# A fused attention and gated feed-forward kernel: the fillings between attention steps dealt anew, and three element-wise jobs moved from VectorE to GpSimd

## What is computed

```
paths  = sigmoid(x @ Wp + bp)                      # 8 heads x 5 values
agree  = pq * pk + (1 - pq) * (1 - pk)
sim    = cumprod(agree, -1).sum(-1) / 5, causal    # 1024 x 1024 per head
x1     = layernorm(x + softmax(sim) @ (x @ Wv) @ Wo)
h      = silu(x1 @ wg.T) * (x1 @ wu.T)             # hidden width 768
out    = layernorm(x1 + h @ wd.T)
```

## Time and profile before

| what | us |
|---|---|
| median of three runs | 982.97 |
| lowest and highest | 975.43, 983.63 |
| the profiled execution's own time | 978.61 |
| its span, first to last instruction | 976.9 |

### The profile page before, as it was taken

The page is one execution under the profiler, slowest core; times in us unless marked ns, Lnnn a source line. Parts: engine busy times, 40 slices in busy tenths (PEclk is TensorE's granted clock), DMA queues, the critical chain, the costliest instruction groups (busy, mean ns, idle before and its releaser), DMA issues.

```text
span 976.9 us, 13193 instructions
## 1 busy us (share of the span) xinstructions
PE 793.5 (81%) x4866; PEld 379.8 (39%) x4866; DVE 737.0 (75%) x1164; ACT 459.7 (47%) x721; POOL 327.3 (34%) x265
## 2 busy tenths in 40 slices
PE   5377798898879889789888889778988888789764
PEld 3133244342533435243443426334443434243332
DVE  2848878779678787797687796797787887788643
ACT  2235554646356454545445463554546463545221
POOL 0010262245324262152512462152622444253412
PEclk9578999999999999999999999999999999999877
DMA  6831443121421424104431415204411224100000
GB/s 206 216 78 52 87 87 108 44 66 44 108 87 44 108 62 108 68 12 97 87 108 44 87 43 121 68 29 108 88 65 44 49 61 108 44 1 22 1 22 23
DMA packets 44338, 70.94 MB, mean 73 GB/s; under 512 B 3568, under 2 KB 21232, under 8 KB 44272
## 3 DMA queue, kind: packets, MB, share of 16 engines
q1 hardware_dynamic: 44272, 70.07, 27.3%
HBM read 53.28 MB, written 16.78 MB: 72 GB/s over the span
## 4 chain that ended last, share of the span: by engine, by line
PE 46%; DVE 21%; issue 11%; ACT 10%; POOL 9%; DMA 2%; SPq 0%; DVEq 0%; ACTq 0%; POOLq 0%
PE misc L808 9%; PE ctx_ps L755 8%; ACT probs L422 7%; PE slot L735 7%; PE misc L711 6%; PE misc L798 6%; PE misc L775 5%; POOL probs L365 5%; DVE acc L508 4%; DVE work L586 4%; POOL work L374 3%; DVE x L569 2%; DVE acc L511 2%; DVE bn L558 2%; PE misc L720 2%
## 5 line engine op out<-in xcount | busy, mean ns | idle before, releaser
L422 ACT ACTIVATE probs<-slot 128x1024 f32<-128x1024 f32 (+3 forms) x384 | 290.3, 809 | 339.9 <-PE slot L735 262.2
L511 DVE TENSOR_TENSOR acc<-acc,probs 128x2048 f32<-128x2048 f32 (+3 forms) x128 | 221.4, 1730 | 5.3 <-POOL probs L365 4.8
L374 POOL TENSOR_TENSOR work<-work 128x512 f16<-128x512 f32 x96 | 145.3, 1514 | 208.8 <-ACT work L440 208.5
L365 POOL TENSOR_SCALAR_AFFINE_SELECT probs<-probs 128x512 f32<-128x512 f32 x128 | 132.5, 1037 | 244.2 <-ACT probs L422 244.2
L735 PE MATMUL slot<-query_stack,key_stack 128*128 128x512 f16 (+3 forms) x768 | 164.4, 337 | 24.9 <-DMA query_stack<-phi_dram 15.2
L755 PE MATMUL ctx_ps<-probs,vz_sb 128*32 128x512 f32 (+3 forms) x1536 | 175.4, 531 | 2.6 <-POOL probs L365 2.6
L798 PE MATMUL misc<-x1T_hi,w_parts 128*128 128x512 f16 x384 | 148.6, 387 | 21.5 <-DVE work L586 15.8
L798 PE MATMUL misc<-x1T_lo,w_parts 128*128 128x512 f16 x384 | 147.5, 384 | 0.0
L735 PEld LDWEIGHTS slot<-query_stack,key_stack 128*128 128x128 f16 x768 | 57.6, 99 | 207.1 <-issue 150.0
L808 PE MATMUL misc<-w_parts,work 128*128 128x256 bf16 x768 | 98.6, 290 | 22.4 <-POOL work L374 22.2
L370 POOL TENSOR_TENSOR rstd<-var_eps,neg_half 128x4 f32<-128x4 f32 x32 | 51.1, 1597 | 182.7 <-DVE var_eps L563 159.2
(11 more groups left out here) (54 smaller groups left out, 636.6 us busy)
## 6 DMA issues: line engine op xcount, KB each, us to landing
key_stack<-phi_dram SPq DMA_DIRECT2D x64, 256.0 KB, 5.8
query_stack<-phi_dram SPq DMA_DIRECT2D x64, 256.0 KB, 6.7
xT_sb<-in_xT_dram SPq DMA_DIRECT2D x8, 1024.0 KB, 5.0
x_sb<-in_x_dram SPq DMA_DIRECT2D x8, 1024.0 KB, 5.6
out_dram<-x SPq DMA_DIRECT2D x16, 512.0 KB, 2.9
phi_dram<-phi_hi SPq DMA_DIRECT2D x16, 256.0 KB, 2.1
phi_dram<-phi_lo SPq DMA_DIRECT2D x16, 256.0 KB, 2.4
work<-in_wgT_dram SPq DMA_DIRECT2D x1, 768.0 KB, 8.2
```

What stands on the lines that cost most here:

```text
L365: pool.affine_select(out=tile, in_=tile, compare_op=ALU.is_ge, fill=0.0, base=0, pattern=[[0, 4], [1, P]], channel_multiplier=-1).then_inc ...
L374: pool.tensor_tensor(hid_lo[:, n % M1, :], hid[:, n % HSLOTS, :], hid_hi[:, n % M1, :], ALU.subtract).then_inc(hid_lo_ready, 1)
L422: act.activation(probs[:, s % P_SLOTS, 2 * p:2 * p + 2, off:CH], slot[p][:, :, off:CH], ACT.Exp).then_inc(slot_drained[p], 1)
L511: dve.tensor_tensor(acc[:, :, off:CH], acc[:, :, off:CH], own, ALU.add).then_inc(summed, 1)
```

## The change

The table `BETWEEN` is rewritten, and `bias`, `features` and `apply` move from VectorE's program to GpSimd's, in the same form of instruction. Since `features` now shares no engine with what follows `turn_f`, it gains a wait, for the transposes of the sample before. The gate pairs stood in steps 7 to 10, 12, 13 and 17 to 22; they now stand in 0 to 2, 12 to 15, 17, 18 and 21 to 23.

```diff
-        0: [("stack", 0, 1)] + down(-1, 0, 0),
-        1: down(-1, 0, 1) + norm(1, -1, 0),
-        2: vz(1, 0, 1, 2) + [("apply", 1, -1, 0), ("store", -1, 0)],
-        3: project(-1, 1) + norm(0, -1, 1),
-        4: vz(1, 3, 4, 5) + [("load_x", 0), ("apply", 0, -1, 1), ("bias", 1, 0), ("squash", 1, 0)],
-        5: vz(1, 6, 7) + [("features", 1, 0)],
-        6: turn_x1(-1, 1) + [("load_xT", 2), ("bias", 1, 1), ("squash", 1, 1)]
-            + turn_f(1, 0, 0) + turn_f(1, 1, 0) + [("features", 1, 1)],
-        7: gate_pair(-1, 6),
-        8: gate_pair(-1, 7) + halves(-1, 6) + turn_f(1, 0, 1) + [("phi_store", 1, 0)],
-        9: gate_pair(-1, 8) + halves(-1, 7) + turn_f(1, 1, 1) + [("phi_store", 1, 1)],
-        10: gate_pair(-1, 9) + halves(-1, 8),
-        11: project(0, 0) + halves(-1, 9) + norm(0, 0, 0),
-        12: gate_pair(-1, 10) + [("apply", 0, 0, 0)],
-        13: gate_pair(-1, 11) + halves(-1, 10),
-        14: turn_x1(0, 0) + halves(-1, 11),
-        15: down(-1, 1, 0),
-        16: [("stack", 1, 0)] + down(-1, 1, 1) + norm(1, -1, 1),
-        17: gate_pair(0, 0) + [("apply", 1, -1, 1), ("store", -1, 1)],
-        18: gate_pair(0, 1) + halves(0, 0),
-        19: gate_pair(0, 2) + halves(0, 1),
-        20: gate_pair(0, 3) + halves(0, 2),
-        21: gate_pair(0, 4) + halves(0, 3),
-        22: gate_pair(0, 5) + halves(0, 4),
-        23: halves(0, 5),
+        0: [("stack", 0, 1)] + gate_pair(-1, 3) + halves(-1, 2),
+        1: gate_pair(-1, 4) + halves(-1, 3),
+        2: gate_pair(-1, 5) + halves(-1, 4),
+        3: vz(1, 0, 1) + halves(-1, 5),
+        4: project(-1, 1) + norm(0, -1, 1),
+        5: down(-1, 0, 0) + [("apply", 0, -1, 1)],
+        6: down(-1, 0, 1) + norm(1, -1, 0),
+        7: vz(1, 2, 3) + [("load_x", 0), ("bias", 1, 0), ("squash", 1, 0), ("apply", 1, -1, 0), ("store", -1, 0)],
+        8: turn_x1(-1, 1) + vz(1, 4) + [("features", 1, 0)],
+        9: vz(1, 5, 6),
+        10: vz(1, 7) + turn_f(1, 0, 0) + turn_f(1, 1, 0)
+            + [("load_xT", 2), ("bias", 1, 1), ("squash", 1, 1), ("features", 1, 1)],
+        11: project(0, 0) + norm(0, 0, 0),
+        12: gate_pair(-1, 6) + [("apply", 0, 0, 0)],
+        13: gate_pair(-1, 7) + halves(-1, 6),
+        14: gate_pair(-1, 8) + halves(-1, 7),
+        15: gate_pair(-1, 9) + halves(-1, 8),
+        16: turn_f(1, 0, 1) + turn_f(1, 1, 1) + halves(-1, 9) + [("phi_store", 1, 0), ("phi_store", 1, 1)],
+        17: [("stack", 1, 0)] + gate_pair(-1, 10),
+        18: gate_pair(-1, 11) + halves(-1, 10),
+        19: turn_x1(0, 0) + halves(-1, 11) + down(-1, 1, 0),
+        20: down(-1, 1, 1),
+        21: gate_pair(0, 0) + norm(1, -1, 1),
+        22: gate_pair(0, 1) + halves(0, 0) + [("apply", 1, -1, 1), ("store", -1, 1)],
+        23: gate_pair(0, 2) + halves(0, 1),
...
+            def features(b, h):
+                rows = slice(HT * H * h, HT * H * (h + 1))
+                pool.wait_ge(u_ready, 2 * b + h + 1)
+                if b == 0:
+                    pool.wait_ge(consts_ready, 3)
+                else:
+
+                    for g in range(NG):
+                        k, n = MISC["turn_f", b - 1, g, h]
+                        pool.wait_ge(misc_filled[k], n + 1)
+                for m in range(DEPTH):
+                    w = 2 ** m
+                    if m >= 1:
+                        pool.wait_ge(feat_ready, DEPTH * (2 * b + h) + m)
+                    pool.tensor_tensor(feat[:, rows, w:2 * w], feat[:, rows, 0:w],
+                                      u_sb[:, rows, m:m + 1].to_broadcast([P, HT * H, w]),
+                                      ALU.mult).then_inc(feat_ready, 1)
+
+            def apply(ln, b, c):
+                pool.wait_ge(rstd_ready, NORM[ln, b, c] + 1)
+                for t in range(TC):
+                    row = x1[:, TC * c + t, :]
+                    pool.tensor_scalar(row, row, mv[:, t, 0:1], rstd[:, t:t + 1],
+                                      ALU.subtract, ALU.mult).then_inc(ln_done, 1)
```

More of the change, by code:

```diff
@@ L370, in rsqrt, with bias_add @@
                 pool.tensor_tensor(rstd[:, :], var_eps[:, :], neg_half[:, :], ALU.pow).then_inc(rstd_ready, 1)
+            def bias_add(b, h):
+                for t in (HT * (h + 1) - 2, HT * (h + 1) - 1):
+                    k, n = MISC["vz", b, t]
+                    pool.wait_ge(misc_drained[k], n + 1)
+                pool.tensor_tensor(z_sb[:, HT * h:HT * (h + 1), :], vz_sb[:, b % 2, HT * h:HT * (h + 1), D:VZ],
+                                  bp_sb[:, :].rearrange("p (a n) -> p a n", a=1).to_broadcast([P, HT, HD]),
+                                  ALU.add).then_inc(z_ready, 1)
+            def features(b, h):
[20 more added lines that the diff above has]
+                                      ALU.subtract, ALU.mult).then_inc(ln_done, 1)
             def hidden_lo(b, n):
@@ L381, in _ @@
                     rsqrt(*n)
+                elif what == "bias":
+                    bias_add(*n)
+                elif what == "features":
+                    features(*n)
+                elif what == "apply":
+                    apply(*n)
                 elif what == "hid_lo":
@@ L563, in stats @@
                 dve.tensor_scalar(var_eps[:, :], mv[:, :, 1], EPS, None, ALU.add).then_inc(var_ready, 1)
-            def apply(ln, b, c):
-                dve.wait_ge(rstd_ready, NORM[ln, b, c] + 1)
-                for t in range(TC):
-                    row = x1[:, TC * c + t, :]
-                    dve.tensor_scalar(row, row, mv[:, t, 0:1], rstd[:, t:t + 1],
-                                      ALU.subtract, ALU.mult).then_inc(ln_done, 1)
             def x1_low(b, c, k2):
@@ L663, in _ @@
                     constants()
-                elif what == "bias":
-                    bias_add(*n)
-                elif what == "features":
-                    features(*n)
                 elif what == "phi":
@@ L679, in _ @@
                     stats(*n)
-                elif what == "apply":
-                    apply(*n)
                 elif what == "split_x1":
```

17 lines of the change are left out of this document (removed).

## The result

| | before | after |
|---|---|---|
| median of four runs, us | 982.28 | 1072.62 |
| lowest and highest | 975.43, 983.63 | 1071.84, 1073.60 |
| span of the profiled execution | 976.9 | 1071.4 |
| mean granted clock over the span | 0.933 | 0.892 |
| mean of the six middle samples | 112.4 | 125.8 |

The change made the kernel slower: the ratio is 1.094, with a 95% interval of 1.088 to 1.099. The forecast was 939, with 912 to 986 as its range.

A forecast was written before the change was run, and what follows sets the result against it. TensorE was taken to set the pace, waiting on VectorE. Middle samples -35, first -5, last -6, tail -5, start +2, configuration +5 made -44: 934.6 against the profiled 978.6, 939 against the median; range 912 to 986.

The forecast's parts named there:

- The price of `apply`: On GpSimd, 0.5 us an instruction of 256 elements, between 0.32 and 1.0; four make 2.0 us.
- So in sum GpSimd is covered: GpSimd's load per sample goes from 40.6 to 56 us, at upper ends 74, well under TensorE's 107.
- rival D: GpSimd's queue becomes the bound in narrow steps 21 to 3, making the kernel slower: 1005 us, chance 0.15.
- Step 19: Transposes, last `halves` and first `down` meet: TensorE gap of 3.8 us before `down`, between 2.5 and 6, with low clock.
- Step 8: Gap of 3.0 us before `vz(1,4)`, between 1.0 and 5.0, from step 7's chain on GpSimd and ScalarE, with low clock.
- Start: Before the first stacks: `bias` and `features` are slower on GpSimd, so 2 us are lost.
- The change of configuration: GpSimd reconfigures near the second sample's `bias` at the start: 5 us charged, bounds 0 and 8.
- First sample: Three gate pairs fewer in the first sample: 5 us saved.
- Last sample: The same gaps go in the last sample, with no `vz` or transposes filling it: 6 us saved.
- Tail: After the last sample, moved gate pairs and `down` blocks fill TensorE's waits: 5 us gained, 0 to 8.
- Rivals B: The gaps nearly all close, step 7's chain hidden and configuration free: 103.2 us a sample, 908 us, chance 0.10.
- C: TensorE's relief is mostly given back, gaps only renamed, 5.0 us in step 8: 976 us, chance 0.17.

The follow-up runs named there:

- e2: The kernel before with the new table `BETWEEN` only; `bias`, `features` and `apply` stay on VectorE: 1011.96 us, ratio 1.032.
- e1: The changed kernel with `apply` back on VectorE; `bias` and `features` stay on GpSimd: 1041.15 us, ratio 1.062.
- e14: e2 with both `down` blocks a step later, `bias` and `features` on GpSimd, `bias` and `squash` of one half a step later: 976.91 us, ratio 0.996.
- e13: e2 with both `down` blocks a step later and `bias` alone on GpSimd: 996.06 us, ratio 1.015.
- e12: e2 with both `down` blocks a step later and the gate pair of step 2 swapped with the `vz` of step 3: 950.49 us, ratio 0.969.
- e3: The kernel before, old table kept, with `bias`, `features` and `apply` on GpSimd: 1063.26 us, ratio 1.084.
- e8: The kernel before with eight added filler matmuls, their results overwritten, ahead of step 0's `down`: 975.68 us, ratio 0.996.

## Why the prediction was wrong

**The price of `apply`: the mis-sized term.** The prediction took 0.5 us an instruction, between 0.32 and 1.0. It measured 1.22 alone and 1.52 on average, above the upper end. The lower bound came from half a mask and the middle value from the low half's rate per element; both assumed that a two-step operation on one tensor goes at the rate of other GpSimd instructions. The upper end, the power on 128x4, was the nearest in kind (1.01 us for almost no elements) and still too low, as it says nothing of the cost per element. GpSimd's load was then 70.8 us in the sample, near the 74 that the prediction gave for all upper ends. The lower end of 9 us for the added work is a slip: its own bounds give 2 x (2.7 + 0.36) + 16 x 0.32 = 11.2.

**"So in sum GpSimd is covered": the step that failed.** The sum was covered even at 70.8 of 126 us. But the engines take their work in order. Four `apply` instructions, 5.8 to 7 us in all, stand between masks that VectorE and TensorE want within one narrow step of 3.5 us. The prediction had rival D for this, with the deciding price of 1.1 us (it was passed) and with `acc` waiting for masks as its sign (74.3 us, seen). What D had wrong: masks and low halves did not lengthen; their means are 837 and 1236 ns, where the groups of before have 1037 and 1514. D counted a sum once more, that of steps 21 to 3, and so arrived at 1005 (with its own 1.6 and 2.0 kept, its 32 us come to 7 x 2.0 + 6 x 2.2 + 3.6 = 30.8, which makes it about 997). The damage there is single waits (3.96 us before the add of step 0, then a TensorE gap of 3.74), and the costliest came in steps 12 to 15, at which D did not look.

**No term for gaps in steps 0 to 3 and 13 to 15: failed, even without GpSimd.** e2 has gaps of 2.15, 0.58, 2.55, 1.63 and 1.75 us in steps 0, 1, 3, 13 and 14. The prediction's sum has nothing for these steps. The gap-by-gap working removed each old gap by its cause and asked of the new table only what each engine has to do per step. It did not ask in which order VectorE comes to the gated products, which is behind the add.

**Step 19: the gap right, its clock wrong.** 3.8 us were forecast; 2.64 + 0.81 came. The stretch of low clock was charged as that of the kernel before, 1.7 us. But this gap is followed by a whole `down`: 5.30 us instead of 2.79, 2.5 lost in that block alone. The prediction had two stretches of 3.4 us at 0.50 in a sample, where before had three; the sample of the changed kernel has one of 3.4 and three of 6.8, 23.8 us in all. In the whole kernel that is the 33.8 us of longer matmuls.

**Step 8: at its upper end.** Forecast 3.0, between 1 and 5; measured 5.03. The chain was the one described: power, mask, `bias`, exponentials, split; the power took 1.94 us, where 1.0 was taken. The table alone has 2.95 there, so the 3.0 were right for VectorE and the `bias` chain on GpSimd is the difference; it was listed among the bounds and not taken.

**The ends.** Start: +2 forecast, +1.3 measured. The change of configuration: 5 forecast between 0 and 8; 7.33 us of idle time before the first `bias` in the changed kernel, and the first sample of e1 6.6 us longer than that of e2. First sample, table alone: -5 forecast, -8.8 in e2. Last sample: -6 forecast, +2.4 in e2. Tail: -5 forecast, +2.1 in e2 and +4.3 in the changed kernel. The tail's gain was argued from gaps that the moved work would fill; the new order made others, such as 4.51 us before a gate pair and 3.52 before the transposes that wait for `apply`.

**What held.** VectorE's load (78 forecast, 81.3), the price of `features` (3.2, and 3.18 to 3.20 alone) and `bias` (0.45, and 0.51), the disappearance of the gap before step 0's `down` and of the two of 1.26, and the largest gaps in step 8 and before step 19's `down` as far as the table alone goes. Rivals B (908) and C (976) are refuted as times; of C's picture the 5.0 us in step 8 came. The step from 106.9 us a sample to a comparable 106.6 is loose: against its own count of 113 the gain is 6.1, not 5.8, which is 2 us in the sum.

**Which engine for element-wise work.** The Trainium skill (GPSIMD Engine Reference, "4.1 Engine selection") sends element-wise work to VectorE. The prediction set it aside, since even at twice the price the sum was covered. The runs agree with the advice: `apply` is 2.6 times as long there (1.22 against 0.47 us), and it costs 31 or 83 us depending on the table. But the Trainium skill puts its factor of about two on two-input operations and calls one-input ones roughly line-rate. `apply` reads one tensor, so the measured 2.6 differs from what that section says, and the measurement decides.

## What to carry to other kernels

Before moving work to a half-idle engine, read what stands behind it in that engine's queue and who waits for it within the length of one step; a share of busy time doesn't answer this, and one move in the order was worth 54 us here. An operation that the engine has not yet run in the trace has no upper bound from other kinds of operation, so the price from which the verdict turns should carry more chance. When fillings are dealt anew, check for each one which other engine still holds its buffer and behind what that release is queued, and count each gap with the matmuls that follow it at the lower clock.

## What the runs showed of the hardware

- On GpSimd a `tensor_scalar` with two operations is dearer per element than a subtraction of two tensors: 1.07 us with constants and 1.22 with operands from memory for 256 elements (4.2 and 4.8 ns each), against 1.15 us for 512 (2.2 ns each). A cost of starting does not explain it: an addition of two tensors of 160 elements took 0.51 us, and an estimate on the line from that to 1.15 for 512 gives 0.7 us for 256.
- VectorE's `tensor_scalar` was held up by GpSimd too. Timeline of e2, four `apply` instructions while GpSimd works without a pause on two masks and two low halves, and then with one mask of 0.63 us beside the first of them:

```profile
596.67 3.37 DVE L569 TENSOR_SCALAR x<-x,mv,rstd 128x256 f32<-128x256 f32 x4
...
640.61 1.68 DVE L569 TENSOR_SCALAR x<-x,mv,rstd 128x256 f32<-128x256 f32 x4 [0.67 <-POOL rstd L370]
```

  The Trainium skill (SBUF — State Buffer, "Who interferes with whom") names `tensor_scalar` among the VectorE instructions that can take the port pair shared with GpSimd; the doubling is in line with that. The single mask in the second case cost nothing to be seen: 1.68 is 4 x 0.42, and the median of e2 is 0.41.
- The change of GpSimd's configuration ahead of the first `bias` shows as 7.0 to 7.4 us of idle time without a releaser (6.98 in e14, 7.43 in e13). The Trainium skill (GPSIMD Engine Reference, "2.1 Instruction dispatch") gives about 6 us for the first call after new code is loaded; the measured time is 1 us or more above it.
- The same 4866 matmuls kept TensorE busy between 778.9 us (e12, clock 0.956) and 838.3 us (e3, clock 0.879), a spread larger than the 44 us that were forecast as gain. The traces show that it is the clock: the busy time less half of what fell on the lower level is 742 to 750 us in every kernel of the table but e8, which has added matmuls.
